# The output bias of an attention layer: from GpSimd's addition to a product on TensorE

## The reference

```python
h = x_tokens @ W_tok + position_table                   # 29 features -> 128 channels
z = layernorm(h)
q, k, v = z @ Wq + bq, z @ Wk + bk, z @ Wv + bv         # 8 heads of 16
attn = softmax((q @ k.T + causal_mask) / 4)             # 1024 x 1024 a head
h = h + (attn @ v) @ Wo + bo                            # bo: the output bias
z2 = layernorm(layernorm(h)) * scale + shift
# gates choose one of 2 groups, and 2 of its 4 experts, with weights
h = h + shared(z2) + sum of the chosen experts(z2)      # hidden width 256, swiglu
```

## Time and profile before

| | |
|---|---|
| median of 3 runs | 950.03 us |
| the profiled execution: its time | 951.46 us |
| its span, first to last instruction | 949.7 us |
| mean granted TensorE clock | 0.984 of 2.4 GHz |
| TensorE busy | 907.3 us, 96% |
| its weight loader (PEld) busy | 540.7 us, 57% |
| VectorE busy | 786.0 us, 83% |
| ScalarE busy | 596.3 us, 63% |
| GpSimd busy | 374.8 us, 39% |

### The profile page before, as it was taken

One profiled execution on the slowest core, in us unless ns is written; L12 is line 12 of the kernel. 1 busy time (PEld: TensorE's weight loads), 2 busy tenths in 40 slices (PEclk: granted clock), 3 DMA queues, 4 the chain that ended last, 5 costly groups with the idle time before them and its releaser, 6 DMA issues. The chain is left out here.

```text
span 949.7 us, 17664 instructions
## 1 busy us (share of the span) xinstructions
PE 907.3 (96%) x5646; PEld 540.7 (57%) x5646; DVE 786.0 (83%) x2529; ACT 596.3 (63%) x1365; POOL 374.8 (39%) x526
## 2 busy tenths in 40 slices
PE   7788999899999999999999999999999999999996
PEld 7633356356575656457555756466564765555575
DVE  5799988798789888889889889898889998894543
ACT  1335675475857675775766675675767576776644
POOL 3713323323445335343354325344444234332424
PEclk9799999899999999999999999999999999999999
DMA  5231011200111001110102001110110101000000
GB/s 178 59 54 50 20 35 34 65 16 4 34 46 57 10 18 49 38 65 18 35 15 72 26 24 40 45 47 30 38 46 17 47 26 46 26 13 2 12 1 23
DMA packets 45980, 35.19 MB, mean 37 GB/s; under 512 B 10816, under 2 KB 44608, under 8 KB 45760
## 3 DMA queue, kind: packets, MB, share of 16 engines
q1 hardware_dynamic: 43680, 31.97, 10.5%
q10 hardware_dynamic: 2208, 2.10, 1.0%
HBM read 4.28 MB, written 4.19 MB: 9 GB/s over the span
## 5 line engine op out<-in xcount | busy, mean ns | idle before, releaser
L1051 ACT ACTIVATE pt<-bank_p 128x512 f32<-128x512 f32 (+3 forms) x768 | 349.9, 492 | 200.6 <-PE bank_p L576 178.5
L784 DVE CUSTOM_DVE_ANT_0 bank_s<-bank_s,causal 128x384 f32<-128x384 f32 (+3 forms) x512 | 244.3, 505 | 40.0 <-PE bank_s L546 37.2
L546 PE MATMUL bank_s<-k_stack,q_stack 96*128 96x512 bf16 (+3 forms) x768 | 236.0, 333 | 17.4 <-DVE mx L784 8.9
L576 PE MATMUL bank_p<-q_stack,k_stack 99*128 99x512 bf16 (+3 forms) x768 | 229.0, 332 | 6.9 <-ACT pt L1051 5.1
L780 DVE TENSOR_REDUCE mx_far<-bank_s 128x1 f32<-128x512 f32 x256 | 166.0, 682 | 20.6 <-PE bank_s L546 19.2
L1213 POOL TENSOR_SCALAR_AFFINE_SELECT pt<-pt 128x512 f32<-128x512 f32 x128 | 81.1, 636 | 206.7 <-ACT pt L1051 206.5
L594 PE MATMUL bank_w<-pt,v 128*32 128x512 f32 (+3 forms) x1536 | 155.2, 502 | 0.2 <-POOL pt L1213 0.2
L546 PEld LDWEIGHTS bank_s<-k_stack,q_stack 96*128 96x128 bf16 x768 | 72.1, 99 | 131.9 <-DVE mx L784 55.6
L576 PEld LDWEIGHTS bank_p<-q_stack,k_stack 99*128 99x128 bf16 x768 | 72.7, 99 | 117.6 <-ACT pt L1051 69.8
L682 PE MATMUL bank_f<-wex_h,hid_h 128*128 128x512 f32 x256 | 116.4, 455 | 0.8 <-DVE gate L936 0.7
L684 PE MATMUL bank_f<-wex_h,hid_l 128*128 128x512 f32 x256 | 101.4, 396 | 0.0
(11 more groups left out here) (139 smaller groups left out, 1428.9 us busy)
## 6 DMA issues: line engine op xcount, KB each, us to landing
q_stack<-qk_h SPq DMA_DIRECT2D x96, 64.0 KB, 2.6
k_stack<-qk_h SPq DMA_DIRECT2D x84, 64.0 KB, 2.6
q_stack<-qk_m SPq DMA_DIRECT2D x64, 64.0 KB, 2.6
out<-h SPq DMA_DIRECT2D x16, 256.0 KB, 2.4
k_stack<-qk_m SPq DMA_DIRECT2D x56, 64.0 KB, 2.6
q_stack<-qk_l SPq DMA_DIRECT2D x32, 64.0 KB, 2.6
k_stack<-qk_l SPq DMA_DIRECT2D x28, 64.0 KB, 2.4
x_sb<-x_t SPq DMA_DIRECT2D x16, 64.0 KB, 2.4
```

The source lines that it names most:

```text
L546: nc.tensor.matmul(s_bank[s % 2][:, 0:cols], q_stack[0:STACK, half, hd, t % HT * P:(t % HT + 1) * P], k_stack[0:STACK, hd, key_place(i, ha ...
L576: nc.tensor.matmul(p_bank[p % 2][:, q0:HALF], k_stack[:, hd, key_place(i, kt // HT), kt % HT * P:(kt % HT + 1) * P], q_stack[:, half, hd, ...
L784: nc.vector.tensor_tensor_reduce(src, src, causal[:, HALF - cols:HALF], 1.0, -3.0e38, ALU.add, ALU.max, mx[:, u, col:col + 1]).then_inc(s_ ...
L1051: nc.scalar.activation(pt[:, k % PT_SLOTS, j, q0:HALF], p_bank[p % 2][:, q0:HALF], ACT.Exp, scale=0.25).then_inc(exp_done, 1)
```

## The change

The bias no longer touches the residual. It is split once into three 16-bit parts whose sum is the 32-bit value (`split_out_bias`, on GpSimd, ten instructions). They are laid into rows 0, 32 and 64 of `bo_rows`, a tensor of 65 rows with zeros elsewhere, four times side by side, 512 columns in all. `bo_ones` is 65 rows of ones. Each output projection now begins with one product of `bo_ones` and `bo_rows` over the whole bank, and the four projections accumulate onto it. GpSimd's item `v` is gone, with the wait for `hb_made` on VectorE. The memset of `k_stack` moves to the beginning of GpSimd's item `forward_weights`, behind `split_out_bias`. TensorE waits once for the split's ten steps. And the strings of `ORDER` are new: items stand elsewhere among their neighbours.

```diff
     if engine == "pool":
-        return (kind in ("stat1", "v", "stat2", "z2t", "hid", "combine", "constants", "forward_weights")
+        return (kind in ("stat1", "stat2", "z2t", "hid", "combine", "constants", "forward_weights")
...
 ORDER = {
     "pe": (
-        "eeaaaaessessssassssassssssesssstssasssasssssssssspsspptpssspspppswspasppsspwspsasssppwppssaspspwsspappss"
...
+        "eeaaaaesesssssassssassssssssesstssassssassspsssssspsspspppstsspsssppwppspaswspspasspspsppsaspswpssassppw"
...
     "dve": (
-        "ieaaeaaaaaaaeasesssssssassssassssasessstsssasasssassssssssssassssastssssassssasssssassasssassssasstsssss"
...
+        "eaeiaaaaaaaaesaesssssssasssassssssasesstssssasassassssssssssasssssastsssasssssassssassassassssssastsssss"
...
     "act": (
-        "aaaddfaaiaddppppppppppapppappppapppwppppppppppppawpppppppbpppappppppppppppppapppppppbppppppppfppwpappfpf"
...
+        "iaaaddfaaaddppppppppppppappapppapppppppwppppppppapwppppppbppappppppppppppppappppppppbpppppppfppwpapppfpf"
...
     "pool": (
-        "aiaaafappppaapapappapbpapaabppfpfpppccppccapaappppbbafpfpppbccbaccppffaapappccppcpbcpppapbafafabcpcpbcpp"
...
+        "aiafappppaappappapbppaapbffppppccpcppcpaappppbbaffppppbccbaccpffpaappccppcpbppcppapbaffabpccbpppfcfapacc"
...
     "sp": (
-        "ieedededtdetdtdddttddddtcddtdetddctddtdctdddetddtcdtedctdddeedtddtdctecddtdddtdtddctdddtedcddteteddcddtt"
...
+        "ieededteddtddtddtdtdddetcetddddtdctddtdctdddtedtddectedcdtdeddtddcdttddecteddddtdcdttdddtdcddttddectddet"
...
                     m_free(i, st)
                     if n == 0:
                         pe.wait_ge(w_in2, 10 * 16)
+                        pe.wait_ge(bo_step, BO_STEPS)
+                    nc.tensor.matmul(m_bank[:], bo_ones[:], bo_rows[:].rearrange("p t c -> p (t c)"), start=True, stop=False)
                     for t in range(HT):
                         mm = nc.tensor.matmul(m_bank[:, t * P:(t + 1) * P], ant[:, t * P:(t + 1) * P], wo_sb[:],
-                                              start=True, stop=True)
+                                              start=False, stop=(t == HT - 1))
...
                 if kind == "oproj":
-                    dve.wait_ge(hb_made, n + 1)
                     dve.wait_ge(m_ready, after(i, *st))
...
-                if kind == "v":
-                    pool.wait_ge(z_made, (n + 1) * HT)
-                    mine = h[:, slot(i, half), :, :]
-                    nc.gpsimd.tensor_tensor(mine, mine, bo_sb[:].unsqueeze(1).to_broadcast([P, HT, P]),
-                                            ALU.add).then_inc(hb_made, 1)
-                    if n == 1:
-                        pool.wait_ge(hb_made, 2)
-                        nc.gpsimd.memset(k_stack[STACK:SHIFTED, :, 1:3, :], -1.0).then_inc(other_keys_made, 1)
-                        pool.wait_ge(other_keys_made, 1)
...
+            def split_out_bias():
+                pool.wait_ge(wv_in, 3 * 16)
+                nc.gpsimd.memset(bo_rows[:], 0.0).then_inc(bo_step, 1)
+                nc.gpsimd.memset(bo_ones[:], 1.0).then_inc(bo_step, 1)
+                nc.gpsimd.tensor_copy(bo_h[:], bo_sb[:]).then_inc(bo_step, 1)
+                pool.wait_ge(bo_step, 3)
+                nc.gpsimd.tensor_tensor(bo_sb[:], bo_sb[:], bo_h[:], ALU.subtract).then_inc(bo_step, 1)
+                pool.wait_ge(bo_step, 4)
+                nc.gpsimd.tensor_copy(bo_m[:], bo_sb[:]).then_inc(bo_step, 1)
+                pool.wait_ge(bo_step, 5)
+                nc.gpsimd.tensor_tensor(bo_sb[:], bo_sb[:], bo_m[:], ALU.subtract).then_inc(bo_step, 1)
+                pool.wait_ge(bo_step, 6)
+                nc.gpsimd.tensor_copy(bo_l[:], bo_sb[:]).then_inc(bo_step, 1)
+                pool.wait_ge(bo_step, 7)
+                for n, part in enumerate((bo_h, bo_m, bo_l)):
+                    row = slice(32 * n, 32 * n + 1)
+                    nc.gpsimd.tensor_copy(bo_rows[row, :, :], part[row, :].unsqueeze(1).to_broadcast(
+                        [1, HT, P])).then_inc(bo_step, 1)
+                pool.wait_ge(bo_step, BO_STEPS)
+
             def split_forward_weights():
+                split_out_bias()
+                nc.gpsimd.memset(k_stack[STACK:SHIFTED, :, 1:3, :], -1.0).then_inc(other_keys_made, 1)
+                pool.wait_ge(other_keys_made, 1)
                 pool.wait_ge(wsplit_h, 1)
```

More of the change, by code:

```diff
@@ L35 @@
 SHIFTED = STACK + 3
+BO_ROWS = 65
+BO_STEPS = 10
 EPS = 1e-5
@@ new lines @@
+        "hspspwwsppsasssppsfssfsswspstpwppssasssswpspsessptswspsppbpspspssppsspsppspppspsbssswwssbwssbspwspappwps"
+        "ppsbsppwssbsfpsspfppfspswpstfpwpfpssfsfsspafsfppssfppssbwsbsfbssppfssbpsfssbpsspfppstsppwwphspwpbsswpbpp"
+        "sappfpfppfpbwwpfsppfepspfsppwsppwppsfpspsfpspasppfppfspsapsfphssfpspstfswwwspspfbsspfpsbfpspsbfspsbsppsf"
+        "psawpwssppwwppsaspspwpspstpsppeppswwppsbspswspsaspsffbspfpsafspfsppwpfsspfpfwspspbfsbpspfbssppfbfpssbspf"
+        "psphwsspfbpsspwwsppstfspsfpfppssbppssfpsspfpsfspapswwspspfswsppftspwpspwpsfasspfpspsfpsapssfspsapssfbpsp"
@@ new lines @@
+        "fsshspsfstfssfppsespfswwwwsppsapssppwpspspassppsswspspssppswssppwpspbspsppwppsspbpwpspstppswpspbsppswsbp"
+        "pspspepspspwppaspspwsppwbpswsspbppfspsfssppfapwwpbfsfbpfssbpfppsfbspfbpspfsppshspfpsbfssftssfpssbsppsfsp"
+        "sapsffpssaswwwwspspfppfssptpfsspasppfsfpspsaspsfpspsfspspwwwwsppsfsbppsfpsspfspsphpsspwssfsppstfpssffpss"
+        "fssppesswwwpspsbspspsppbspspwppbpspwspsbpspspwwpeppssppasppwspsppwsptspwpspbswssassffspapfpsfsbpspffassp"
+        "pfspswpspfwpssbfsbfbspspfbspfbpspsfpphspspfbpswwpssptwspsfspbspspfppsapspfpspswpspswwsppfpfssppftssppfsp"
@@ L166 @@
+        "wppsbsspwspsasppfspswpstfpspbfpsspasppswspfsppswwppssbfpaspspfpspfspspfppsswssppwwspsfppssfppsfstfsppsfp"
+        "ssfspphppsswwssppswpssfsspfsppbpspswspbppspsbppssbppwpwssptwsppwppsspsppwsppsppbspswpssbsppsffwsppfwpspf"
+        "fsppfsspfspsfspspfpssfspsfsppsfppsfpptfpbwwppbwppbpwppwpbpwpbppwpphppwppbpwpbppfppfppwppffppwppffwppfppf"
+        "ppbffwwfbfbfbbfhbffffbffffffffbffffhffff"
     ),
     "dve": (
[L168 removed]
@@ new lines @@
+        "sasssfasssfshssstssfsseafssasssssssasssassbsssbssstssssbsbsassbassssssbsbbsbfsfbbffsbsfsfssffsbbssbhsfss"
+        "sssbstfbssebabssssbfssasfssassfsfsasfstssfssassfsfssssssafsfstssfssshssfssssfsssssfesassssssabssbsssasss"
+        "ssbssbtssbsasssssssasfsfssbfssfebssfbsfsbfabsfsssbabfssssafssshssstssbfsbssfbasssssssassftfssbssbssbbsba"
+        "ssfsfsfssfssssssfsassfsfsssssfstsshsssssfssssfssbssbsssssbbstsssssbssssssbssbfsbfbfbfssfssfssfssfsssfsss"
+        "fsstbbbbbhfbfbbbffffffffbbfbbbhbfffbfbfbffffbffbffhff"
@@ L204 @@
+        "dcdtddtddctdtdtcccc"
     ),
@@ L269, in build @@
         bv_sb, bo_sb = sb("bv_sb", [P, P]), sb("bo_sb", [P, P])
+        bo_h, bo_m, bo_l = (sb(n, [P, P], BF16) for n in ("bo_h", "bo_m", "bo_l"))
+        bo_rows, bo_ones = sb("bo_rows", [BO_ROWS, HT, P], BF16), sb("bo_ones", [BO_ROWS, P], BF16)
         bgate_sb = sb("bgate_sb", [P, NGATE])
@@ L348, in build @@
         stat1, mv_made, var_made, rs_made = sem("stat1"), sem("mv_made"), sem("var_made"), sem("rs_made")
-        z_made, hb_made = sem("z_made"), sem("hb_made")
+        z_made, bo_step = sem("z_made"), sem("bo_step")
         zth_made, zt_made = sem("zth_made"), sem("zt_made")
```

77 lines of the change are left out of this document (27 added, 50 removed).

## The result

The changed kernel takes 952.16 us, the median of 20 runs (949.6 to 953.56); the kernel before takes 950.75 us in the same comparison (20 runs). The ratio is 1.0016, 95% interval [1.0009, 1.0023]: 1.5 us slower, by less than the 0.3% set as the bound. Forecast were +3.8 us.

What follows compares the result with a forecast made beforehand. TensorE was taken as the bound, busy 641.12 of 650 us from 200 to 850 us. Terms 2.9 + 0.6 + 0.3 = +3.8 us on the median of 950.03 gave 953.8 us, range 946.5 to 959.5.

Steps and rivals of the forecast that it cites:

- Part 1: On GpSimd, sixteen bias additions of 1.29 us go; nobody waited for them, so 0 gained.
- Part 2: On TensorE, one more product per half, sixteen at 0.22 us, mostly uncovered: +2.9 us, between 0 and 7.0.
- The discount of 0.4: On TensorE after 200 us, products replace loader waits for exponentials or maxima in 13% of the time: minus 0.4 us.
- Part 3: At the start, GpSimd's bias steps delay its long product, which holds VectorE's cast longer: +0.6 us, between 0 and +4.
- rival C: Worse start: bias steps take 8 us, 957.8, or collide with the normalization at 24.9, 1.6 us, 955.4; chance 0.12.
- Part 4, the start: On VectorE, the weights' split moved ahead pushes the normalization to 12.4, past the bank being free at 12.12: +0.3 us.
- Part 4, SyncE's queue: Transfers move by a place or two; an x tile or store has many us of air: 0.
- Part 4, the weave: The rewoven order is neither tighter nor looser by counts of runs of scores and probabilities: 0, 4 us either way.
- Rival A: The new weave clears loader waits for exponentials and maxima, 16 of 199 for 0.3% faster; 20 give 945.6; chance 0.21.
- Rival B: TensorE takes the added product into its holes, little of the 2.9 us is left: 951.3 us; chance 0.22.

Runs made afterwards that it cites:

- experiment 5: The changed kernel without the sixteen bias products, the parts still made on GpSimd: 948.2 us, -2.9 against the kernel before, -4.4 against the changed kernel.
- experiment 1: The changed kernel in the order of items of the kernel before: 955.5 us, +4.0 against the kernel before.
- 9: The changed kernel in the old order, with the constant rows of `k_stack` written at ScalarE's start: 950.58 us, -0.3 against the kernel before.
- 4: The changed kernel with four bias products per projection instead of one, 48 more: 961.1 us, +10.2 against the kernel before, 8.7 against the changed kernel.
- 6: The changed kernel with ScalarE writing the constant rows of `k_stack` in place of GpSimd's memset: 949.06 us, -2.6 against the kernel before.
- experiment 8: The kernel before in the new order, additions kept on GpSimd, `k_stack` rows written by ScalarE: 946.4 us, -5.4 against the kernel before.
- experiment 3: The changed kernel with the bias steps and `k_stack` memset behind the weights' low parts on GpSimd: 949.29 us, -1.9 against the kernel before.
- experiment 10: The changed kernel with the new order for the first 100 us, the old order after: 957.7 us, +7.1 against the kernel before.
- experiment 11: The changed kernel with the old order for the first 100 us, the new order for the rest: 949.31 us, -1.1 against the kernel before.
- experiment 7: The kernel before, additions and GpSimd's order kept, `k_stack` rows written at ScalarE's start instead of by GpSimd's memset: 945.64 us, -6.3 against the kernel before.

## Why the prediction was right, and where its terms were wrong

The time came out where it was forecast to lie, +1.5 us instead of +3.8, and on the other side of the 0.3% from the one I held likelier. It did so with one term of zero that was worth -2.5, another that cost several times its price, and a third that was right. That the sum came out near is in part luck: the two wrong terms lie on opposite sides.

**Part 1, the addition costs nothing where it stood: stands as a reading.** Nobody waits for `bo_sb` in either trace. No run took the addition away by itself.

**Part 2, the product: +2.9 forecast.** Distance, count and cover were as forecast: 0.22 us, sixteen, nobody waits for `bo_rows`. What it is worth in time has four readings: 4.4 (within 1.5) for all sixteen in experiment 5, 2.0 and 3.9 us for the last fourteen in the traces of 1 and 9, and 0.18 us for each further one in 4, which would make 2.9 for sixteen. My 2.9 lies within them. The discount of 0.4 in it, that a product takes the place of a wait of the loader, isn't seen: these waits are 81.8 us before and 82.6 in experiment 1. That the first product of a projection costs more than a further one (0.27 against 0.18) is suggested, not shown; the intervals overlap.

**Part 3, the parts and the memset: +0.6 forecast, mis-sized.** The times on GpSimd's side were right to a tenth (28.9 and 42.7), by two errors that cancel: the ten steps took 4.64 us and not 4.2, and began at 24.21 and not at 24.66. VectorE's side wasn't. I let the cast start at 40.2; it started at 39.20, since the start was a microsecond faster than I thought (below), and so it lost 3.4 us, not 2.4, to a product whose end did not move. A cast that comes sooner to the same end gains nothing. The price had to be read from the ends: cast and subtraction are done at 44.67 in the changed kernel and at 44.71 in experiment 1 instead of 43.14, which is GpSimd's whole delay of 1.5 us in both orders and not 0.6. In the old order (experiment 1) cast and subtraction together lost 1.48 + 4.18 = 5.7 us instead of 2.7, and the same exponential was 2.8 us later at 78 us. Less the two products that lie before 205 us, where it was 2.7, this term was some +2.4 there, four times my price and inside the bounds of 0 to +4; what makes 2.4 out of the 1.5 isn't shown. GpSimd's next statistics, which I expected about 1 us later than 59.76, stand at 62.27, 2.5 later. Parts 2 and 3 together, 3.5 forecast, have five readings (overlapping ones): 4.0, 3.6, 2.9 (6 minus 8), 6.0, and 4.4 without the start; the middle one is 4.0.

The normalization beside the bias's steps, named under rival C, took 1.59 us instead of 1.11, and 1.38 to 1.85 in six other traces with these steps beside it; in experiment 3, where the steps come later, it is 1.11 again. In the changed kernel that is 0.5 us of the 1.6 that four whole steps would have cost. The Trainium skill (SBUF — State Buffer, "SBUF: two separate sides") says that if VectorE works in a two-port mode, or with two inputs in SBUF while the GpSimd instruction reads SBUF, whichever of the two engines starts first has the shared ports for its whole instruction. This case's traces agree for the long instructions: the cast that starts inside one of GpSimd's ends 0.3 us after it, be it a product (42.73, then 43.00) or a memset (50.23, then 50.51). In which mode the cast runs no trace says.

**Part 4, the start: +0.3 forecast, wrong.** I had the four instructions of the split push the normalization. In the new trace they fit ahead of it: the embedding's addition goes at 8.55 and the split at 9.16 to 10.03, and the normalization starts at 10.06, when the statistics are there. ScalarE's first copy is at 11.94 instead of 12.93. I had read TensorE's row of the embedding before, at 7.65 and 2.05 long, as the time at which the bank is ready, and put the addition there; in the new trace and in that of experiment 1, whose order here is the old one, the same eight products have 1.13, and in the new trace the addition starts 0.10 us behind their end. Of the microsecond, 0.34 is an earlier first load; the three experiments in which that load came as before (4, 8, 10) have the copy at 12.28, so the order gives 0.65. In the changed kernel it is lost again at the cast.

**Part 4, SyncE's queue: 0 forecast, wrong.** I wrote that transfers are moved by a place or two with many us of air. They were not all so. SyncE's queue before, near the first image's second half:

```profile
35.36 1.82 SPq L440 DMA_DIRECT2D q_stack<-qk_h  x3
41.50 1.19 SPq L440 DMA_DIRECT2D q_stack<-qk_m  x2
43.16 0.55 SPq L440 DMA_DIRECT2D q_stack<-qk_l  x1
45.93 0.57 SPq L449 DMA_DIRECT2D q_stack<-mrow_h  x1
```

and after, with the score of TensorE that waited:

```profile
47.30 0.57 SPq L452 DMA_DIRECT2D q_stack<-mrow_h  x1
...
49.18 0.58 SPq L420 DMA_DIRECT2D x_sb<-x_t  x1
49.80 1.87 SPq L443 DMA_DIRECT2D q_stack<-qk_h  x3
...
52.98 0.59 SPq L443 DMA_DIRECT2D q_stack<-qk_l  x1
53.62 1.89 SPq L443 DMA_DIRECT2D q_stack<-qk_h  x3
```

```profile
57.48 0.60 PE L549 MATMUL bank_s<-k_stack,q_stack 96*128 96x512 bf16 x2 [1.02 <-DMA q_stack<-qk_l]
```

Before, the queries' parts went out as they came, the high ones at 35.36 and the low one at 43.16, ahead of the maxima's rows. In the new order they are behind three transfers of maxima and an x tile: the high parts at 49.80, the low one at 52.98, and TensorE waits 1.02 us for it at 57.48. Its place in the queue is only part of that: it also landed 4.5 us after its issue, the one of before 2.3 us after. This wait is in the traces of seven of the eight kernels that begin with the new order (not in experiment 3), 0.6 to 4.6 us long, and in none of the six that begin with the old one. In experiment 3 the same transfer goes out at 48.45 and lands 2.6 us later, in time; in experiment 8 it goes out at 48.44 and lands 6.3 us later, which makes the 4.59 us of wait. So it is a likely part of the new start's +3.1 in experiment 10, whose trace has it with 1.6 us, and of the gains that didn't add in 8; no run moved these transfers alone.

The rest of that loss I can't settle. After against before, the same exponential is 0.9 us later at 57 us, 3.8 at 78, 5.6 at 147, then 1.3 at 205 and 0.1 at 400. From 60 to 110 us, before and after (columns as in rows 1):

```profile
60.00:110.00 50.00, 45.78 (x264) 17.79 (x264) 44.65 (x139) 30.25 (x65) 16.23 (x22) 0.93 0.10 33
```

```profile
60.00:110.00 50.00, 46.01 (x241) 17.41 (x240) 42.92 (x129) 26.66 (x57) 12.86 (x18) 0.83 0.16 40
```

TensorE ran at a mean clock of 0.93 before and 0.83 after. Between 19 and 100 us it stood at 1.2 GHz for 20.5 us before and for 34.1 us after. The additional 13.6 us at half rate would be enough for the loss, but no run separated the clock from the holes around it. It isn't a matter of these two executions alone: over the whole span the mean granted clock has its median at 0.9785 in the twenty runs of the changed kernel, and at 0.982 to 0.985 in the three sets of 23 runs of the kernel before that the experiments were timed against.

**Part 4, the weave: 0 within 4 forecast, -2.5 and -2.1 measured.** Counting runs of three and more in the strings told nothing of its sign. Rival A had the sign, and part of the mechanism. By its own sign, 16 vanished waits, it fails: 4 vanished. But the waits got shorter: the loader's waits for exponentials and maxima from 200 to 850 us sum to 80.4 to 82.6 us in the five traces with the old rest and to 75.4 to 77.7 us in the nine with the new one, with the product and without it. How much of that reaches the end isn't shown. Ahead of this stretch, about 3 us of the better rest are made from 180 to 208 us, where the trace of experiment 11 lacks the low clock that the one of experiment 1 has; why it is lacking there isn't shown. Rival B's figure, 951.3, is nearer to the result than the forecast's own, and its reason is refuted by experiments 4 and 5.

## What to carry to other kernels

Ask of every moved transfer which score or product reads it and what now stands ahead of it in its queue: "moved by a place or two" is no price. When VectorE and GpSimd both work on SBUF in a start, look for the long GpSimd instructions, memsets too, and give their work to an engine that idles; here 6.3 us lay in that, four times what the change under study did. And a total that comes out right proves none of its terms: here +4.0 and -2.5 hid behind +1.5.

## What the runs showed of the hardware that I had not expected

- A GpSimd memset of 3 partitions, 6.92 us long, held VectorE's cast from 32-bit to 16-bit for 5.14 us instead of 0.42 (experiment 3).
- The same eight products of the embedding stand in the trace with 2.05 us before and with 1.13 in experiment 1, at the same clock and 0.03 us apart in their start: the length of such a row is a poor measure of when its bank can be read.
- Removing a stall of 2.7 us on VectorE near 40 us made the whole 6.3 us faster (experiment 7): the stall's echo in TensorE is 3.14 us, and what makes up the rest isn't settled.
- A stretch of 6.83 us at 1.2 GHz near 180 us is in seven of the fourteen traces, and with it about 3 us: in all five with the old rest, in two of the nine with the new one.
- The same transfer, issued at 48.4 us, landed 2.6 us later in experiment 3 and 6.3 us later in experiment 8.
